# Adding one tile of partial sums to the other by an accumulating DMA instead of VectorE, and a bias folded into a matmul

## The reference, cut to what matters

```python
delta = softplus(x_dbl[..., :64] @ dt_w.T + dt_b)      # 256 channels
def step(h, ins):                                      # over 256 tokens, 16 states per channel
    h = h * exp(d_t[:, :, None] * A) + (d_t * u_t)[:, :, None] * B_t[:, None, :]
    y = einsum('bds,bs->bd', h, C_t)
y = ys + xm * D_ssm
y = y * silu(res)
return y @ out_w.T + out_b
```

## Time and profile before

| what | value |
|---|---|
| median of three runs | 1661.06 us |
| profiled execution, its own time | 1652.15 us |
| its span in the profile | 1650.3 us |
| VectorE busy | 1392.8 us (84%) |
| TensorE busy | 1308.1 us (79%) |
| ScalarE busy | 1276.0 us (77%) |
| GpSimd busy | 650.3 us (39%) |
| DMA queue of GpSimd, time of its packets over 16 engines | 38.6% |
| granted TensorE clock, mean over the span | 0.899 |

### The profile page before, as it was taken

One profiled execution on the slowest core, in us unless ns is written; L12 is line 12 of the kernel. 1 busy time (PEld: TensorE's weight loads), 2 busy tenths in 40 slices (PEclk: granted clock), 3 DMA queues, 4 the chain that ended last, 5 costly groups with the idle time before them and its releaser, 6 DMA issues. The chain is left out here.

```text
span 1650.3 us, 29068 instructions
## 1 busy us (share of the span) xinstructions
PE 1308.1 (79%) x8642; PEld 1175.9 (71%) x8642; DVE 1392.8 (84%) x2151; ACT 1276.0 (77%) x2660; POOL 650.3 (39%) x681
## 2 busy tenths in 40 slices
PE   7977568878888687878888688878888787667788
PEld 6867557767778686767778687777777676457678
DVE  3367899989899888989989898989989898988742
ACT  3489658978888787978889698978879698549722
POOL 1212435273624436273534536263533534242210
PEclk9989668989999799999989799998979899678889
DMA  6336347675666667665666767665665765455631
GB/s 199 115 87 140 75 84 158 145 178 125 163 147 143 144 142 180 150 161 121 158 149 142 167 136 185 140 164 111 152 154 134 175 150 106 83 136 113 159 89 45
DMA packets 144230, 227.02 MB, mean 138 GB/s; under 512 B 13648, under 2 KB 79440, under 8 KB 143952
## 3 DMA queue, kind: packets, MB, share of 16 engines
q0 software_dynamic: 39424, 123.76, 38.6%
q1 hardware_dynamic: 104656, 101.41, 21.2%
HBM read 90.90 MB, written 25.17 MB: 70 GB/s over the span
## 5 line engine op out<-in xcount | busy, mean ns | idle before, releaser
L984 ACT ACTIVATE dA<-delta,A 128x255 f32<-128x255 f32 x1024 | 425.7, 495 | 5.3 <-DVE hs L1354 4.4
L1360 DVE TENSOR_TENSOR_SCAN hs<-dA,b_r 128x512 f32<-128x512 f32 x256 | 297.5, 1201 | 14.3 <-PE b_r L671 11.5
L1354 DVE TENSOR_TENSOR_SCAN hs<-dA,dbu 128x1024 f32<-128x1024 f32 x128 | 292.9, 2288 | 17.1 <-ACT dA L984 11.1
L1372 DVE TENSOR_TENSOR G<-hs,b_r 128x1024 f32<-128x1024 f32 x192 | 233.3, 1215 | 25.5 <-PE b_r L682 19.2
L558 PE MATMUL b_out<-w2s,hT 128*128 x1680 | 238.2, 289 | 19.7 <-ACT ys L905 10.5
L544 PE MATMUL b_h<-xsT,wst 128*128 128x128 f32 x1680 | 242.9, 292 | 10.0 <-ACT hT L913 10.0
L558 PEld LDWEIGHTS b_out<-w2s,hT 128*128 128x128 f32 x1680 | 216.9, 202 | 29.0 <-issue 27.9
L854 ACT ACT_TABLE_LOAD x182 | 233.5, 1283 | 3.9 <-PEq L1760 0.7
L544 PEld LDWEIGHTS b_h<-xsT,wst 128*128 128x128 f32 x1680 | 225.3, 208 | 12.5 <-issue 11.8
L671 PE MATMUL b_r<-prm,scaled 128*128 128x128 f32 x1024 | 172.5, 299 | 58.4 <-ACT scaled L1000 29.1
L1000 ACT ACTIVATE scaled<-duT,dtT 128x256 f32<-128x256 f32 x512 | 217.1, 501 | 0.3
(11 more groups left out here) (181 smaller groups left out, 2244.5 us busy)
## 6 DMA issues: line engine op xcount, KB each, us to landing
wst<-w_dram SPq DMA_DIRECT2D x242, 256.0 KB, 2.9
acc<-G POOLq DMA_DIRECT2D x96, 512.0 KB, 5.1
odd<-G POOLq DMA_DIRECT2D x96, 512.0 KB, 5.3
xsort<-sorted SPq DMA_DIRECT2D x70, 192.0 KB, 5.4
results<-ys SPq DMA_DIRECT2D x70, 192.0 KB, 3.2
odd<-xd POOLq DMA_DIRECT2D x32, 256.0 KB, 3.3
xin<-x_dram SPq DMA_DIRECT2D x8, 256.0 KB, 4.9
sorted<-ys SPq DMA_DIRECT2D x2, 960.0 KB, 7.3
```

Source lines behind the costliest of these rows:

```text
L984: last = do(dA[j % 4][:, d, k, 1:], delta[b][:, k, 1:], ACT.Exp, scale=A[:, k, s:s + 1])
L1354: V.tensor_tensor_scan(flat(hs[j % 2]), flat(dA[j % 4]), flat(dbu[n % 2]), 0.0, ALU.mult, ALU.add)\
L1360: V.tensor_tensor_scan(hs[j % 2][:, d, :, :].rearrange("p h t -> p (h t)"), dA[j % 4][:, d, :, :].rearrange("p h t -> p (h t)"), R[u % 2][ ...
L1372: V.tensor_tensor(to[:, :, :, :], hs[j % 2][:, :, :, :], both(C).unsqueeze(2).broadcast_to([P, DP, HALVES, T]), ALU.mult).then_inc(q_G, 1)
```

## The change

Four edits. (1) The VectorE addition of `odd[b]` to `acc[b]` is gone; a new GpSimd step `w`, first in every slot (and at the head of `finish`), waits for both last landings and issues one more accumulating DMA, `merge`. (2) In slots 0 and 2 the gate moves behind the next step of the VectorE list. (3) The bias `dt_b` becomes a row of `dt_w`, and the copy to `dtT` sets the matching row to one: the copy is split into 256 columns with a bias and 32 without. (4) `z` is gone: one Abs over both halves writes `ez`, and `delta` reads the projection straight from PSUM (`W[1]`).

```diff
     "vector": (
-        "b0 s0 g0 s1 gate g1 b2 s2 g2 s3 low b4 g3 delta s4 g4 s5 b6 mask g5 s6 g6 s7 xb g7",
+        "b0 s0 g0 s1 g1 gate b2 s2 g2 s3 low b4 g3 delta s4 g4 s5 b6 mask g5 s6 g6 s7 xb g7",
...
-        "b0 s0 s1 g0 gate b2 g1 xsum s2 s3 un g2 b4 lx g3 s4 s5 g4 ln b6 low s6 g5 unx delta g6 s7 g7",
+        "b0 s0 s1 g0 b2 gate g1 xsum s2 s3 un g2 b4 lx g3 s4 s5 g4 ln b6 low s6 g5 unx delta g6 s7 g7",
...
     "gpsimd": (
-        "skip a2 a3 a4 a5 a6 a7",
+        "w skip a2 a3 a4 a5 a6 a7",
...
-                do(dtT[b][:, :], W[0][:, 0:T + 2 * DS], ACT.Copy).then_inc(q_dt, 1)
+                do(dtT[b][:, 0:T], W[0][:, 0:T], ACT.Identity, bias=par("one_at"))
+                do(dtT[b][:, T:], W[0][:, T:T + 2 * DS], ACT.Copy).then_inc(q_dt, 1)
...
-                for o, f in ((ez, ACT.Abs), (z, ACT.Identity)):
-                    for k in range(HALVES):
-                        do(o[:, k, :], W[1][:, k * T:(k + 1) * T], f, bias=par("dt_b")[:, k:k + 1])
+                do(ez[:, :, :], both(W[1]), ACT.Abs)
...
-                V.scalar_tensor_tensor(out=delta[b][:, :, :], in0=z[:, :, :], scalar=0.0, in1=ez[:, :, :],
+                V.scalar_tensor_tensor(out=delta[b][:, :, :], in0=both(W[1]), scalar=0.0, in1=ez[:, :, :],
...
             def gate_y(g, i):
                 q, b = 4 * g + i, i % 2
-                dve.wait_ge(*landed(q, 6))
-                dve.wait_ge(*landed(q, 7))
-                V.tensor_tensor(acc[b][:, :, :, :], acc[b][:, :, :, :], odd[b][:, :, :, :], ALU.add)
-                dve.drain()
+                dve.wait_ge(q_sum, (q + 1) * 16)
...
+            def merge(g, i):
+
+                q, b = 4 * g + i, i % 2
+                pool.wait_ge(*landed(q, 6))
+                pool.wait_ge(*landed(q, 7))
+                Q.dma_start(flat(acc[b]), flat(odd[b]), accum_op=ALU.add).then_inc(q_sum, 16)
...
+                    elif name == "w":
+                        if tail:
+                            merge(*tail)
...
             def finish():
                 one, two = slice(0, HALF), slice(HALF, TILES)
                 f = (LAST, xb, ob, GROUPS - 1, False)
+                merge(GROUPS - 1, 3)
                 ffn_root(LAST, one)
```

More of the change, by code:

```diff
@@ L22 @@
         ("out_w", HALVES * D), ("write_w", D), ("read_w", D), ("norm1", 1), ("norm2", 1),
-        ("in_b", 2 * HALVES), ("conv_b", HALVES), ("conv_w", HALVES * DC), ("dt_b", HALVES),
+        ("in_b", 2 * HALVES), ("conv_b", HALVES), ("conv_w", HALVES * DC),
         ("A_log", HALVES * DS), ("D_ssm", HALVES), ("out_b", 1), ("decay", 1), ("dt_w", DI),
         ("out_b_row", D), ("ident", P), ("dist", T), ("causal", T), ("iota", E), ("tap_b", DI), ("ones_row", P),
-        ("outside", PAD), ("before", P), ("steps", TILES), ("tiles", 15), ("ones_e", E), ("sel", 24)]
+        ("outside", PAD), ("before", P), ("steps", TILES), ("tiles", 15), ("ones_e", E), ("one_at", 1), ("sel", 24)]
 DP = 2
@@ L31 @@
 NG = 3
+BIAS_ROW = 2 * DS + DP
 TURNED = (1, 3, 5, 7)
@@ L250, in moe_mamba_kernel @@
         duT = [sb(f"duT{b}", [P, T // P, DI]) for b in range(SEQ)]
-        z = sb("z", [P, HALVES, T])
         ez = sb("ez", [P, HALVES, T])
@@ L1724 @@
     xp = a("attn_x_proj_w")
-    bc = np.concatenate([xp[DR:]] * 2, 0).T
+    bc = np.concatenate([xp[DR:]] * 2, 0).T.copy()
+    bc[:, BIAS_ROW] = 0.0
     ob = a("attn_out_proj_b")
@@ L1731 @@
          np.broadcast_to(taps.reshape(1, -1), (P, DC * DI))], 1))
+    dt_w = np.concatenate([np.zeros((P - DR, DI), f), a("attn_dt_proj_w").T], 0)
+    dt_w[BIAS_ROW] = a("attn_dt_proj_b")
     parts = {
@@ L1740 @@
         "in_b": rows(a("attn_in_proj_b")[:, None]), "conv_w": rows(a("attn_conv_w")[:, 0, :]),
-        "conv_b": rows(a("attn_conv_b")[:, None]), "dt_b": rows(a("attn_dt_proj_b")[:, None]),
+        "conv_b": rows(a("attn_conv_b")[:, None]),
         "A_log": rows(a("attn_A_log")), "D_ssm": rows(a("attn_D_ssm")[:, None]), "out_b": ob[:, None],
         "decay": np.broadcast_to(a("attn_decay").reshape(1, 1), (P, 1)),
-        "dt_w": np.concatenate([np.zeros((P - DR, DI), f), a("attn_dt_proj_w").T], 0), "out_b_row": fill(ob[None, :]),
+        "dt_w": dt_w, "one_at": (np.arange(P) == BIAS_ROW).astype(f)[:, None], "out_b_row": fill(ob[None, :]),
         "ident": np.eye(P, dtype=f), "dist": np.maximum(t - 1 - s, 0).astype(f), "causal": (t > s).astype(f),
```

## The result

The changed kernel is slower. Its median is 1673.42 us (1672.76 to 1677.83, four runs) against 1660.14 us for the kernel before on the same chip, a ratio of 1.0092 with a 95% interval from 1.0071 to 1.0113. The forecast was 1653.7 us and faster. The profiled executions are 1673.63 us after and 1652.15 before, so single traces differ by somewhat more than the medians (1% of this kernel is 16.6 us).

The account below looks back on a forecast made before the run. VectorE was taken as the bound in slots 0 and 2, GpSimd's gathers as setting the end of slots 1 and 3. The terms summed to -7.4 us, from 1661.06 to 1653.7 us; the range, leaving 2 in 10 out, was 1643 to 1667.

Parts of the forecast that it names:

- root behind `merge`, `xd` at `fnorm`, `finish`: GpSimd standing still: late root in slots 3 +6.0, `xd` beside `fnorm` +3.0, later `xn` in `finish` +3.6 us.
- gates of slots 2: Eight slots 2: four keep part of the saved addition, four nothing; gain 2.0 us, bounds 0 and 10.
- ScalarE, `dt` path: 0.5 to 1.4 us a slot come off ScalarE, but VectorE seldom waits for it; gain 1.5 us.
- gates of slots 1 and 3: Slots 1 gain nothing; slots 3, where four lose all to the gathers' wait, gain 3.0 us, bounds 0 and 5.
- Gain 7 x 1.27 - 2.2 = 6.7 us: Slot 0: seven saved additions of 1.27 us, less 2.2 us of gate waits for `merge` to land.
- rival B: No change: VectorE's gains in slots 0 and 2 become waits for TensorE or ScalarE; 1658 to 1664 us, 22%.
- The halving: Late root in six slots 3: 12.6 us if all were like the case shown; half taken, 6.0.
- the root is just in time: 0: Slot 1: `fnorm` stands behind `g0` too, 1.2 us later, so the root behind `merge` costs 0.
- Rival A: Slower: `froot`'s addition in slots 1 and 3 still meets a scan; 1681 us, or 1667 with half; 15%.
- 0.5 us kept: Slot 2, case shown: `xsum` must await the out-projection, so 0.5 of the addition's 1.27 us is kept.
- this is on the path everywhere: `fsum` behind the gathers, no longer beside `xd`: 13 x 0.53 = 6.8 us gained, bounds 0 and 8.
- nothing, as the gathers decide: Slot 1, eight: the saved addition gains nothing, since `fsum` waits for GpSimd's gathers at the slot's end.

Follow-up runs that it names:

- root_first: The changed kernel with the root (`froot`) ahead of `merge` in slots 1, 3 and `finish`: 1650.68 us, ratio 0.9945.
- slot0_add: root_first with slot 0 and `finish` put back to VectorE's addition, the gate at its old place: 1641.03 us, ratio 0.9892.
- slot2_add: root_first with slot 2 alone put back to VectorE's addition, the gate at its old place: 1651.62 us, ratio 0.9961.
- odd_root: The changed kernel with root ahead of `merge`, `merge` only in slots 1 and 3, VectorE's addition at its old places elsewhere: 1642.88 us, ratio 0.9896.
- the warm8 pair: root_first with 8 idle TensorE matmuls (the fill) ahead of slot 2's out-projection, 1648.04 us, ratio 0.9926; paired with slot0_add_warm8.
- dt_only: The kernel before with only the change's `dt` path (bias through the matmul, one Abs, `delta` from PSUM): 1655.93 us, ratio 0.9980.
- root_first_old_dt: root_first with the old `dt` path (`z`, four reads, bias on ScalarE): 1657.20 us, ratio 0.9987.
- xd_later: The kernel before with `xd` in slots 0 and 2 held back until `a7` has landed: 1657.45 us, ratio 0.9991.
- slot0_late: root_first with slot 0's gate one more step later, behind the product `b2`: 1652.14 us, ratio 0.9962.
- slot0_add_warm8: slot0_add with 8 idle TensorE matmuls ahead of the out-projection in slot 2: 1640.41 us, ratio 0.9884.

## Why the prediction was wrong

It forecast -7.4 us, and the ratio gives +15.3, outside its range of 1643 to 1667 us. By its own terms:

| term | forecast us | measured us | by |
|---|---|---|---|
| root behind `merge`, `xd` at `fnorm`, `finish` | +12.6 | +24 | root_first |
| gates of slots 0 (with the merge of `finish`) | -6.7 | +7 to +11 | slot0_add, slot2_add, odd_root, the warm8 pair |
| gates of slots 2 | -2.0 | -2.7 to -0.7, not told from 0 | the first three of these |
| ScalarE, `dt` path | -1.5 | -3.3 to -7.0 | dt_only, root_first_old_dt |
| `xd` off `fsum` | -6.8 | -1.5, not told from 0 | xd_later |
| gates of slots 1 and 3 | -3.0 | about -9 to -12 | remainder, below |

The last line is what odd_root's 1.04% (17.3 us) leaves when the `dt` path and `xd` are taken off; no kernel isolated it. It is the larger where the `dt` path is the smaller. As it is a remainder, the column adds up to about 15.3 by construction, and that is no test of it.

**The step that failed** is "Gain 7 x 1.27 - 2.2 = 6.7 us" for slot 0: wrong in sign, 14 to 18 us off. It had two faults. The waits summed to 7.9 us, not 2.2, in the same seven slots. Part of it is a lag that no row of before showed: by the trace's semaphore events `merge`'s issue starts 0.53 us after `a7`'s last one, in all 32 cases, where the prediction took nothing (3.7 of the missing 5.7 us). And the main fault: it priced only VectorE. The addition saved 8.9 us there and the waits took 7.9, which would have been a small gain. But `yg` comes later, and behind it stand ScalarE's `sres` and `xm` and TensorE's projections for the next tile; slot0_late shows that `yg` can't be delayed further even where VectorE's own wait shrinks. This is the mechanism of rival B, "VectorE's gains in slots 0 and 2 turn into waits for TensorE or ScalarE"; xd_later may show it a second time, with other work. The prediction let the gates in B still gain a few us; that they could lose was in none of its rivals.

**The root** was right as a mechanism and mis-sized. The text took 2.1 us late in half of six slots. Measured: `xn` waits 2.1 to 2.9 us in five of the six and 0.8 in the first, 13 us in all, and 5.2 in `finish`. The halving is what failed: no row stood behind it. (The addition took 0.52 and not 0.19, which was read from a tile of half the width; that is 0.3 us of each wait.) A second payment isn't shown to be the root's. `lg` behind it waited 16.3 us in these six slots and 11.0 before, but in the nine kernels with the root in time it waited 8.1 to 15.6. In odd_root, in the same slot 3 (q = 15), `xn` doesn't wait for the root, and from its start to `lg`'s pass 6.4 us, with a granted clock of 0.54 from 794.0 to 797.7; it is 6.7 us in the changed kernel and 5.0 before. (TensorE idles 2.3 us for ScalarE ahead of `xn` in both odd_root and the kernel before, and in the latter the clock stayed at 1.00, so why it falls in the one and not in the other stays open.) The waits for the root, `finish` (+3.4) and the 3.2 us of `xn`'s time that root_first gave back make 19.5 of the 24 us, which is within what the ratios leave open. In slot 1 "the root is just in time: 0" was right; `finish` with +3.6 was right (+3.4). Rival A had the right place and the wrong cause, the addition that meets a scan: the additions took 0.47 us in the mean. So what the prediction said against A held, and that 1673.4 us lies between A's two prices, 1667 and 1681, is luck.

**Slot 2** agrees in size (-2.0 against -2.7 to -0.7) but not by its step, "0.5 us kept". `yg` waited there for `merge` too (6.5 of the 14.4 us), where the text had it in time, and `x` waited 11.6 us for the out-projection, 0.8 before: 17 us more of waits against 10.2 us of additions (8 x 1.27). By VectorE's list alone that is a loss, so the agreement is luck, or something else gained there that no run isolated.

**`xd`**: "this is on the path everywhere" was wrong. The sums were shorter by 7.9 us, about the 6.8 forecast, and the time wasn't kept. Beside `fnorm` it was forecast to cost 3.0 us in the six slots 3; the `xn` of all slots 3 took 2.3 us more, and those of slots 1, which had no price, 2.5. The Trainium skill, page "SBUF — State Buffer", section "Who interferes with whom", has a rule of mutual exclusion that would have given 5.6 in the six slots 3. The trace doesn't bear that out: in the slot shown the four `xn` grew by 0.40 us beside an `xd` of 0.93.

**Slots 1**: "nothing, as the gathers decide" was too low. `fsum`'s wait for them fell from 3.1 us a slot to 1.9 instead of growing to 4. In the eleven kernels with the merge in slots 1 and 3 it was 9.5 to 14.6 us in all, and 18.6 to 19.1 in the three without, so it goes with the merge. Why the gathers come earlier stays open: in root_first the root's addition took 2.1 us again, and the wait was still 11.4.

**Open.** How slot 0's loss divides between `yg`'s later place, the wait for the landing and the merge's own traffic: a merge with the gate at its old place wasn't tried. What share of it is the low clock behind TensorE's idle time, since the fill was tried only in slot 2. And whether the `dt` path really gives more on top of root_first.

## What to carry to other kernels

Ahead of handing an addition to a queue, ask what stands behind it on the issuing engine: an issue that waits for a landing is a wait for everything after it, and here, to issue the root ahead of the merge turned 0.9% slower into 0.5% faster. Price an operation that comes later by what hangs on its result on the other engines, not by the wait on its own. And decide by slot: the merge seems to have paid in slots 1 and 3 (a remainder, not a test), did little in slot 2 and cost some 9 us in slot 0, so of the best kernels here slot0_add (1.1% under the kernel before; slot0_add_warm8 and odd_root are level with it) uses it in slots 1 to 3 alone.

## What the runs showed of the hardware

- From `a7`'s last semaphore event to the start of the next DMA issue on GpSimd, which waited for it, 0.53 us passed in all 32 cases.
- An accumulation of 512 KB from SBUF into SBUF took 4.5 to 6.2 us from issue to landing, like those before it, though the prediction took the queue to be quiet there.
- Shortly after TensorE had idled for 2.4 us its granted clock fell from 1.00 to 0.61, and the out-projection took 2.9 instead of 1.6 us; with a fill of 1.95 us ahead of it the clock stayed at 1.00. Mending that gave 3 us, which can't be told from nothing. In a slot 0, behind 4.3 us without work, the granted clock was 0.67, and in a slot 3, behind 2.2 us, 0.72 and then 0.50.
- The root's addition on GpSimd (128x4) took 2.14 us where VectorE's scan ran, and 0.52 where VectorE waited.
